# Merging attention's heads: the squares on ScalarE, the three turns of the reciprocal root and the scaled product on GpSimd

## The chip, the cores and the metric

The kernel runs on one core of a Trainium2 chip. The metric is the device time of one execution in microseconds (us). The engines are TensorE (PE, with its weight loads as PEld), VectorE (DVE), ScalarE (ACT), GpSimd (POOL) and SyncE (SP), which only issues transfers here.

## The reference

Two layers, each with a modulated layer norm, an attention-like part and a feed-forward part. Only the first layer's attention matters here: batch 8, 512 tokens, width 128, 16 heads, two softmax maps per head, values 16 wide.

```python
a1 = softmax(where(causal, s1, -inf)); a2 = softmax(where(causal, s2, -inf))
comb = a1 - lam[None, :, None, None] * a2
out = einsum('bhqk,bhkv->bhqv', comb, v)
mu = mean(out, -1); var = mean(square(out - mu), -1)
normed = (out - mu) * rsqrt(var + LN_EPS)
scaled = normed * (1.0 - LAM_INIT)
merged = scaled.transpose(0, 2, 1, 3).reshape(B, S, 2 * E)
return merged @ Wo
```

The kernel takes the mean out of the value weights beforehand, so `mu` is zero and only the mean of the squares is left to compute.

## The kernel before

Attention takes the first half of the execution. It goes in rounds of eight slots, `g` = 0 to 7, one round for each batch. A slot works on several things at once: the first pass of the scores for head pair `g` (matmuls into the banks `p1b`, and for each of ten units a row maximum by VectorE, `bmax`, L1055), the second pass for the pair two slots before (matmuls into `p2b`, exponentials by ScalarE into `pT`, L684), the causal clearing of `pT` by GpSimd (L645, twice a slot: once for blocks of the pair two slots before and once for the last blocks of the pair three slots before), the product with the values for the pair three slots before (`weigh`, L831), and the copying and turning of its result for the pair four slots before (L690, L861, L696).

The three banks `p1b` couple TensorE and VectorE closely: the second pair of units of a slot (units 2 and 3) can only be written once VectorE has read unit 0 of the same slot, the first pair only once it has read unit 8 of the slot before. At the end of a slot VectorE reduces the maxima to `qneg` (L1071). GpSimd splits that into `nsp` (L639, L641), and TensorE turns it in the middle of the next slot (L869, `turn_neg`). The turns all go through one bank, `auxb`, in a fixed order: `turn_neg`, `turn_o`, `value`, and each waits until ScalarE has copied out the one before.

Round r also finishes the batch `pb` = r - 1 ("post"). In slot 3 VectorE takes the reciprocals of the softmax sums (L1017). In slot 4 GpSimd makes the two scaled outputs `og` and `o2` (L655, L656), in slot 5 it adds them (L631). Then VectorE squares them before unit 4 of slot 5 (L1029), sums the squares before unit 8 of slot 5 (L1031), scales the sum and starts the reciprocal root before unit 4 of slot 6 (L1033 and L60 to L62), makes three Newton turns before units 5, 6 and 7 (L66 to L68) and the product `merged` before unit 9 (L1039). Each of the small steps waits for the one before through `Chain.link`. In slot 7 TensorE turns `merged` in two halves (`turn_m0` after the first pair of units, `turn_m1` after `weigh(1)`, L901), ScalarE copies them out (L719), and TensorE multiplies them with `wo` (L908). VectorE adds the gated result to `x` at the start of the next round (L1074, L1078).

On every engine the order is that of the program. GpSimd's order in a slot is: the copy of the values `vs` (L628), the addition of slot 5, `nsp`, the clearing of the last blocks, the post products of slot 4, and at the end of the slot the two clearings that wait for the eighth exponential. `weigh(1)` of the next slot waits for these:

```python
if c == CHUNK_FIRST:
    pe.wait_ge(masked, 2 * G + 2)
```

The last round, r = B = 8, has only post work of batch 7 left and does the whole of it on VectorE (`alone` on GpSimd is true then). Round 0 has no post work. So seven rounds, 1 to 7, have the steps above beside the other work.

Of the kernel before, what the change touches and what calls it, by code (L numbers as in the profile page):

```python
# [16 lines left out]
ALU = mybir.AluOpType  # L17
ACT = mybir.ActivationFunctionType
AX = mybir.AxisListType.X

B, S, D = 8, 512, 128
# [3 lines left out]
VD = 2 * HD  # L25
LAM_INIT = 0.8 - 0.6 * math.exp(-0.3 * 11)
EPS = 1e-5
# [15 lines left out]
class Chain:  # L43
# [6 lines left out]
    def link(self, ins):  # L50
        ins.then_inc(self.sem, 1)
        self.n += 1
        self.eng.wait_ge(self.sem, self.base + self.n)
        if self.passed is not None:
            self.eng.sem_inc(self.passed, 1)
# [376 lines left out]
GROUPS = 8  # L432
# [14 lines left out]
CHUNK_FIRST, CHUNK_LAST = 1, 0  # L447
O_COPY_AT, HIGH_AT, MT_AT, HT_AT, MID_AT, NEG_COPY_AT, OT_AT, V_COPY_AT = 0, 0, (1, 3), 2, 4, 4, 6, 9
RES_AT, NORM_AT = 3, 0
POST_AT = ((3, 9), (5, 4), (5, 8), (6, 4), (6, 5), (6, 6), (6, 7), (6, 9))  # L450
FIRST = ((DIAGONAL, 0), (EDGE, 0), (DIAGONAL, 1), (EDGE, 1), (MIDDLE, None))
BLOCK_STEP, SLOT_STEP, BLOCK_SLOTS, MAP_WORDS = 5, 2, 5, 28

# [35 lines left out]
def aux_use(r, g, kind):  # L489

    return (r + 1) * AUX_USES + AUX_PLACE[g, kind]
# [11 lines left out]
def attention(nc, d, k, t):  # L503
# [3 lines left out]
    with ExitStack() as ctx:  # L507
# [6 lines left out]
        def sem(name):  # L514
            return ctx.enter_context(nc.semaphore(name))
# [15 lines left out]
            sem(n) for n in ("first_unit", "first_read", "second_unit", "exp_done", "masked", "masked_last", "vs_ready", "av_done", "o_read"))  # L531
        qneg_ready, nsp_high, nsp_ready = (sem(n) for n in ("qneg_ready", "nsp_high", "nsp_ready"))
        rc_ready, og_ready, merged_ready, post_done = (sem(n) for n in ("rc_ready", "og_ready", "merged_ready", "post_done"))
        pool_own, dve_post, passed, og_parts = sem("pool_own"), sem("dve_post"), sem("passed"), sem("og_parts")
        f_xn, f_turned, f_hT, f_up, f_arg = (sem("f0_" + n) for n in ("xn", "turned", "hT", "up", "arg"))
        f_hid_tile, f_arg_tile, f_turns_tile = (tile[:, 0, :, :] for tile in ffn_tiles(k))
        f_bank, f_banks = p1b[0], (p1b[1], p1b[2], p2b[0], p2b[1])
# [74 lines left out]
        @block.gpsimd  # L612
        def _(pool):
            for s, n in CREDITS.items():
                pool.sem_inc(s, n)
            def slot(r, g, on, prep, post):
                pb = r - 1
                o = oT[:, (r + 1) % 2, :, :, 0:VD].rearrange("p c (h j) e -> p (c h) j e", j=2)
                rcv = rc[:, :, :, :].rearrange("p c h j -> p (c h) j")
                full = [P, TILES * H, VD]  # L620
                alone = isinstance(r, int) and r == B
                if on(2):
                    r2, g2 = lagged(r, g, 2)
                    G = r2 * GROUPS + g2
                    a = g2 % 2
                    pool.wait_ge(aux_read, aux_use(r2 - 1, 6, "value") + 1)
                    pool.wait_ge(av_done, G + 1)
                    pool.tensor_copy(vs[:, a, :, :, :], vst[:, r2 % 2, :, 2 * g2:2 * g2 + 2, :]).then_inc(vs_ready, 1)  # L628
                if post and g == 5 and not alone:
                    pool.wait_ge(pool_own, pb * 2 + 2)  # L630
                    pool.tensor_tensor(og[:, :, :], og[:, :, :], o2[:, :, :], ALU.add).then_inc(og_ready, 1)  # L631
                if on(1):
                    rn, gn = lagged(r, g, 1)
                    G, a = rn * GROUPS + gn, gn % 2
                    high, mid = (nsp[:, a, :, :, s, :].rearrange("p c j h -> p (c j) h") for s in range(2))
                    lowest = qneg[:, a, :, :].rearrange("p c (j h) -> p (c j) h", j=2)
                    pool.wait_ge(qneg_ready, G + 1)
                    pool.wait_ge(aux_done, aux_use(*lagged(r, g, 2), "turn_neg") + 1)
                    pool.tensor_copy(high, lowest).then_inc(nsp_high, 1)  # L639
                    pool.wait_ge(nsp_high, G + 1)  # L640
                    pool.tensor_tensor(mid, lowest, high, ALU.subtract).then_inc(nsp_ready, 1)  # L641

                def clear_future(pairs, n, signal):

                    pool.affine_select(out=pairs, in_=pairs, compare_op=ALU.is_ge, fill=0.0, base=0,  # L645
                                       pattern=[*n, [1, P]], channel_multiplier=-1).then_inc(signal, 1)

                if on(3):
                    r3, g3 = lagged(r, g, 3)
                    pool.wait_ge(exp_done, (r3 * GROUPS + g3 + 1) * UNITS + BANK_CREDITS)  # L650
                    clear_future(pT[:, g3 % 2, 8:10, :].rearrange("p n (a t) -> p (n a) t", a=2)[:, :, 0:P], [[0, 4]], masked_last)
                if post and g == 4 and not alone:
                    pool.wait_ge(rc_ready, pb + 1)
                    pool.wait_ge(merged_ready, pb + 1)
                    pool.tensor_tensor(og[:, :, :], o[:, :, 0, :], rcv[:, :, 0].unsqueeze(2).broadcast_to(full), ALU.mult).then_inc(pool_own, 1)  # L655
                    pool.tensor_tensor(o2[:, :, :], o[:, :, 1, :], rcv[:, :, 1].unsqueeze(2).broadcast_to(full), ALU.mult).then_inc(pool_own, 1)  # L656
                if prep and 1 <= g < 5:
                    j, J = g - 1, (r + 1) * 4 + g - 1
                    pool.wait_ge(mid_ready, J + 1)
                    pool.tensor_tensor(parts[:, j % 2, 2, :], res, parts[:, j % 2, 1, :], ALU.subtract).then_inc(split_ready, 1)  # L660
                if on(2):
                    r2, g2 = lagged(r, g, 2)
                    a = g2 % 2
                    pool.wait_ge(exp_done, (r2 * GROUPS + g2) * UNITS + 8 + BANK_CREDITS)
                    clear_future(pT[:, a, 0:8, 0:P], [[0, 8]], masked)
                    clear_future(pT[:, a, 1:8:2, 384:512], [[0, 4]], masked)

            rounds(pool, slot)

        @block.scalar  # L670
        def _(act):
            act.wait_ge(factor_ready, 1)

            def slot(r, g, on, prep, post):
# [6 lines left out]
                for u in range(UNITS):  # L681
# [22 lines left out]
                    if u == MID_AT and prep and 1 <= g < 5:  # L704
                        j = g - 1
                        act.wait_ge(aux_read, aux_use(r, g, "project") + 1)
                        act.activation(parts[:, j % 2, 1, :], res, ACT.Copy).then_inc(mid_ready, 1)
                    if u == NEG_COPY_AT and on(1):
                        rn, gn = lagged(r, g, 1)
                        act.wait_ge(aux_done, aux_use(r, g, "turn_neg") + 1)  # L710
                        if not isinstance(rn, int) or rn * GROUPS + gn >= 2:
                            rp, gp = lagged(rn, gn, 2)
                            act.wait_ge(neg_loaded[gp % RING], (use(rp, gp) + 1) * NEG_LOADS)
                        act.activation(nparts[:, gn % 2, :], auxb[0:2 * MAPS, 0:S // 2].bitcast(BF16), ACT.Copy).then_inc(aux_read, 1)
# [255 lines left out]
        def _(dve):  # L970
            fill = Chain(dve, dve_fill).link

            def slot(r, g, on, prep, post):
# [33 lines left out]
                        split_b2(dve, fill, k)  # L1007
                full = [P, TILES * H, VD]
                wide = lambda t: t[:, :].unsqueeze(2).broadcast_to(full)
                at = dict(zip(POST_AT[1:7], (0, 1, 2, 6, 9, 12)))  # L1010
                for u in range(UNITS):
                    if post and (g, u) in at:
                        link = Chain(dve, dve_post, pb * POST_LINKS + at[g, u]).link
                    if post and (g, u) == POST_AT[0]:
                        dve.wait_ge(aux_read, aux_use(r, POST_AT[0][0], "turn_o") + 1)
                        dve.wait_ge(og_ready, pb + 2)
                        dve.reciprocal(rc[:, :, :, :].rearrange("p c h j -> p c (h j)"), oT[:, (r + 1) % 2, :, :, VD]).then_inc(rc_ready, 1)  # L1017
                        if isinstance(r, int) and r == B:
# [5 lines left out]
                                dve.tensor_tensor(to[:, :, :], o[:, :, j, :], rcv[:, :, j].unsqueeze(2).broadcast_to(full), ALU.mult).then_inc(og_parts, 1)  # L1024
                            dve.wait_ge(og_parts, 2)
                            dve.tensor_tensor(og[:, :, :], og[:, :, :], o2[:, :, :], ALU.add).then_inc(og_ready, 1)
                    if post and (g, u) == POST_AT[1]:
                        dve.wait_ge(og_ready, pb + 3)
                        link(dve.tensor_tensor(sq[:, :, :], og[:, :, :], og[:, :, :], ALU.mult))  # L1029
                    if post and (g, u) == POST_AT[2]:  # L1030
                        link(dve.tensor_reduce(vsum[:, :], sq[:, :, :], AX, ALU.add))  # L1031
                    if post and (g, u) == POST_AT[3]:
                        link(dve.tensor_scalar(vsum[:, :], vsum[:, :], 1.0 / VD, EPS, ALU.mult, ALU.add))  # L1033
                        rsqrt_start(dve, link, vsum[:, :], vhalf[:, :], orstd[:, :], otmp[:, :])
                    if post and (g, u) in POST_AT[4:7]:
                        rsqrt_newton(dve, link, vhalf[:, :], orstd[:, :], otmp[:, :])
                    if post and (g, u) == POST_AT[7]:
                        dve.wait_ge(aux_done, aux_use(r - 1, GROUPS - 1, "turn_m1") + 1)
                        dve.scalar_tensor_tensor(merged[:, :, :].rearrange("p c (h e) -> p (c h) e", e=VD), og[:, :, :], 1.0 - LAM_INIT,  # L1039
                                                 wide(orstd), ALU.mult, ALU.mult).then_inc(merged_ready, 1)  # L1040
                    if on(0):
                        t, j = divmod(u, 2)
                        kind, head = FIRST[t]
# [36 lines left out]
            rounds(dve, slot)  # L1080


POST_LINKS = 3 + RSQRT_LINKS


def token_stats(dve, link, k, batches):
# [1378 lines left out]
```

## Time and profile before

| what | value |
|---|---|
| median of 3 runs | 1449.06 us (1448.51 to 1450.49) |
| profiled execution | 1447.97 us, span 1446.2 us |
| attention in the trace | from about 57 us to about 680 us |
| PE / DVE / ACT / POOL busy over the span | 83% / 80% / 74% / 55% |
| mean granted clock of TensorE | 0.939 |

The profiled execution lies 1.09 us below the median of the runs. 1.8 us of it lie outside the span. The shares of busy time are averages over stages with different limits; the rows below come from single slots of attention.

### The profile page before, as it was taken

The page shows a single profiled execution, that of the slowest core. Times are in us where ns is not written, and L with a number is a line of the kernel's source. Part 1 is how long each engine was busy: PE and PEld are TensorE (multiplying, and loading weights), DVE is VectorE, ACT ScalarE, POOL GpSimd, SP SyncE. Part 2 cuts the span into 40 slices and gives each one's busy share as a digit, 9 for nine tenths or more (in the row PEclk, how much of TensorE's full clock was granted, in tenths as well). Part 3 has the DMA queues.
Part 4 walks back from the last instruction along what each step waited for, and adds up shares of the span by engine and source line. Part 5 has one row for each costly group of instructions (what it writes and reads, how often), then busy time and mean ns, then how long its engine had stood idle before and what let it go on. Part 6 is the DMA issues. An engine that isn't in the chain of part 4 may idle for free. (4 is left out here: it accounts for less than half of the span.)

```text
span 1446.2 us, 26470 instructions
## 1 busy us (share of the span) xinstructions
PE 1200.6 (83%) x8837; PEld 562.0 (39%) x8837; DVE 1156.0 (80%) x2000; ACT 1072.2 (74%) x1712; POOL 801.6 (55%) x721
## 2 busy tenths in 40 slices
PE   4489989898989898876876678787669999999998
PEld 3234443434444444333544223232234444444443
DVE  5678988888888888886776999999947776777653
ACT  2178878787878787874976888885467788778775
POOL 3134636362636363530001699899637787777777
PEclk8589999999999999996898899998889999999999
DMA  5341414141414141100003798988578677767884
GB/s 134 101 133 55 135 36 143 35 141 39 137 42 136 44 133 46 57 3 0 1 0 97 242 298 312 300 284 283 177 157 186 174 193 179 192 174 184 191 199 120
DMA packets 123690, 198.63 MB, mean 137 GB/s; under 512 B 24604, under 2 KB 60088, under 8 KB 123576
## 3 DMA queue, kind: packets, MB, share of 16 engines
q1 hardware_dynamic: 122136, 195.08, 47.4%
q10 hardware_dynamic: 1440, 2.10, 0.5%
q8 instruction: 64, 1.05, 0.3%
q14 instruction: 50, 0.41, 0.1%
HBM read 167.76 MB, written 28.84 MB: 136 GB/s over the span
## 5 line engine op out<-in xcount | busy, mean ns | idle before, releaser
L1055 DVE TENSOR_REDUCE bmax<-p1b 128x4 f32<-128x512 f32 x640 | 406.9, 685 | 64.0 <-PE p1b L760 58.2
L684 ACT ACTIVATE pT<-p2b 128x512 f32<-128x512 f32 x640 | 349.3, 599 | 97.5 <-PE p2b L813 97.3
L2203 POOL TENSOR_TENSOR hid_l<-e_hid,w_experts 128x1024 f16<-128x1024 f32 (+1 forms) x136 | 281.1, 2083 | 104.5 <-ACT w_experts L2338 103.6
L645 POOL TENSOR_SCALAR_AFFINE_SELECT pT<-pT 128x512 f32<-128x512 f32 (+1 forms) x192 | 148.0, 787 | 201.9 <-ACT pT L684 201.9
L2437 DVE TENSOR_TENSOR e_hid<-ub,w_experts 128x1024 f32<-128x1024 f32 x128 | 155.8, 1223 | 121.7 <-ACT ub L2349 113.1
L831 PE MATMUL ob<-pT,vs 128*32 128x384 f32 (+3 forms) x2048 | 185.7, 447 | 8.3 <-ACT o_sb L690 6.5
L1906 PE MATMUL yb<-ch,ident 128*128 128x512 f32 x256 | 134.5, 655 | 45.8 <-POOL ch L1876 45.5
L2338 ACT ACTIVATE w_experts<-e_hid 128x1024 f16<-128x1024 f32 (+1 forms) x136 | 139.4, 1026 | 38.3 <-DVE e_hid L2437 38.2
L2349 ACT ACTIVATE ub<-ub 128x1024 f32<-128x1024 f32 (+1 forms) x136 | 133.9, 985 | 37.6 <-PE ub L2254 35.9
L760 PE MATMUL p1b<-w_high 48*128 48x128 bf16 (+2 forms) x1792 | 129.0, 246 | 37.3 <-DVE bmax L1055 37.1
L813 PE MATMUL p2b<-w_high 50*128 50x512 bf16 (+3 forms) x1024 | 124.8, 301 | 2.4 <-ACT pT L684 1.9
L1986 ACT ACTIVATE dA<-dt,nA 128x511 f32<-128x511 f32 x128 | 85.5, 712 | 46.7 <-DVE hs L2049 34.7
L2252 PE MATMUL ub<-w,w_high 128*128 (+1 forms) x264 | 100.9, 382 | 22.2 <-DVE e_hid L2437 12.9
L760 PEld LDWEIGHTS p1b<-w_high 48*128 48x128 bf16 x1792 | 63.4, 96 | 115.6 <-DVE bmax L1055 97.7
L1876 POOL TENSOR_TENSOR ch<-hs,crow 128x1024 f32<-128x1024 f32 x40 | 93.9, 2353 | 12.6 <-DVE hs L2049 12.5
L2253 PE MATMUL ub<-w,w_high 128*128 (+1 forms) x264 | 100.8, 382 | 0.0
L2254 PE MATMUL ub<-w,w_low 128*128 (+1 forms) x264 | 100.8, 382 | 0.0
L2252 PE MATMUL e_yb<-w_experts,w_high 128*128 128x512 f16 x264 | 100.1, 379 | 0.5 <-POOL hid_l L2203 0.5
L2254 PE MATMUL e_yb<-w_experts,w_low 128*128 128x512 f16 x264 | 100.1, 379 | 0.0
L2253 PE MATMUL e_yb<-hid_l,w_high 128*128 128x512 f16 x264 | 100.1, 379 | 0.0
L1906 PEld LDWEIGHTS yb<-ch,ident 128*128 128x128 f32 x256 | 47.2, 200 | 121.7 <-POOL ch L1876 76.3
L2049 DVE TENSOR_TENSOR_SCAN hs<-dA,dBx 128x1024 f32<-128x1024 f32 x40 | 91.4, 2284 | 3.4 <-ACT dA L1986 0.6
(308 smaller groups left out, 2150.4 us busy)
## 6 DMA issues: line engine op xcount, KB each, us to landing
w_experts<-shares SPq DMA_DIRECT2D x256, 256.0 KB, 4.3
brow<-bc_rows SPq DMA_DIRECT2D x64, 512.0 KB, 4.0
crow<-bc_rows SPq DMA_DIRECT2D x64, 512.0 KB, 5.3
q_stacks<-w_low SPq DMA_DIRECT2D x96, 128.0 KB
k_stacks<-w_low SPq DMA_DIRECT2D x96, 128.0 KB
w_high<-q_stacks SPq DMA_DIRECT2D x128, 96.0 KB, 2.4
w_high<-k_stacks SPq DMA_DIRECT2D x128, 96.0 KB, 2.3
w_high<-nparts SPq DMA_DIRECT2D x128, 4.0 KB
```

Source lines behind the costliest of these rows:

```text
L645: pool.affine_select(out=pairs, in_=pairs, compare_op=ALU.is_ge, fill=0.0, base=0, pattern=[*n, [1, P]], channel_multiplier=-1).then_inc(s ...
L684: act.activation(pT[:, g2 % 2, stored(u), :], p2b[bank_of(g2, u)][:, :], ACT.Exp, scale=SCALE).then_inc(exp_done, 1)
L760: return pe.matmul(bank[:, at * P:(at + blocks[1] - blocks[0]) * P], qs[rows, slot, head, c * P:(c + 1) * P], ks[rows, slot, head, blocks[ ...
L831: mm = pe.matmul(ob[32 * m:32 * m + 32, q0:q1], vs[:, a, c, m // 2, :], pT[:, a, u, at:at + q1 - q0], start=(c == CHUNK_FIRST), stop=(c == ...
L1055: dve.tensor_reduce(to, bank, AX, ALU.max).then_inc(first_read, 1)
L1906: mm = pe.matmul(yb[:, :], k.ident[:, :], ch[:, m % 4, j, :], start=False, stop=(m == PAIRS - 1 and j == 1), skip_group_check=True)
L2203: pool.tensor_tensor(flat(hid_l[:, rounded(p), 0:n, :]), flat(hid[:, place(p), 0:n, :]), rounded_half(p, 0, n), ALU.subtract).then_inc(spl ...
L2252: pe.matmul(to, w[0], high, start=start, stop=False, skip_group_check=True)
L2253: pe.matmul(to, w[0], low, start=False, stop=False, skip_group_check=True)
L2254: return pe.matmul(to, w[1], high, start=False, stop=stop, skip_group_check=True)
L2338: act.activation(rounded_half(p, 0, n), flat(hid[:, place(p), 0:n, :]), ACT.Copy).then_inc(hid_rounded, 1)
L2437: dve.tensor_tensor(h, u, flat(share[:, p % SHARES, :, :]), ALU.mult).then_inc(hid_ready, 1)
```

## The change

ScalarE squares `og` in slot 5 after its fifth exponential (`SQ_AT`). VectorE sums the squares before unit 7 of slot 5, and scales the sum and starts the root before unit 9 of slot 5. GpSimd makes the three turns, as twelve chained instructions instead of nine, and the product, in slot 6 between the clearing of the last blocks and the two clearings at the end. The factor 1 - LAM_INIT goes into the scale of the sum, so that the last product is a plain one. The last round keeps everything on VectorE, at other places of the program but in the same sequence.

```diff
-POST_AT = ((3, 9), (5, 4), (5, 8), (6, 4), (6, 5), (6, 6), (6, 7), (6, 9))
+SQ_AT = 4
+RC_AT, SUM_AT, START_AT, MERGE_AT = (3, 9), (5, 7), (5, 9), (6, 6)
+MERGE_SCALE = (1.0 - LAM_INIT) ** -2
...
+                if post and g == 6 and not alone:
+                    pool.wait_ge(dve_post, (pb + 1) * POST_LINKS)
+                    link = Chain(pool, pool_newton, pb * NEWTON_LINKS).link
+                    for _ in range(3):
+                        link(pool.tensor_tensor(otmp[:, :], orstd[:, :], orstd[:, :], ALU.mult))
+                        link(pool.tensor_tensor(otmp[:, :], otmp[:, :], vhalf[:, :], ALU.mult))
+                        link(pool.tensor_scalar(otmp[:, :], otmp[:, :], 1.5, None, ALU.add))
+                        link(pool.tensor_tensor(orstd[:, :], orstd[:, :], otmp[:, :], ALU.mult))
+                    pool.wait_ge(aux_done, aux_use(r - 1, GROUPS - 1, "turn_m1") + 1)
+                    pool.tensor_tensor(merged[:, :, :].rearrange("p c (h e) -> p (c h) e", e=VD), og[:, :, :],
+                                       orstd[:, :].unsqueeze(2).broadcast_to(full), ALU.mult).then_inc(merged_ready, 1)
...
+                    if post and (g, u) == (5, SQ_AT) and not (isinstance(r, int) and r == B):
+                        act.wait_ge(og_ready, pb + 3)
+                        act.activation(sq[:, :, :], og[:, :, :], ACT.Square).then_inc(sq_ready, 1)
...
-                    if post and (g, u) == POST_AT[1]:
-                        dve.wait_ge(og_ready, pb + 3)
-                        link(dve.tensor_tensor(sq[:, :, :], og[:, :, :], og[:, :, :], ALU.mult))
-                    if post and (g, u) == POST_AT[2]:
+                    if post and (g, u) == SUM_AT:
+                        dve.wait_ge(sq_ready, pb + 1)
                         link(dve.tensor_reduce(vsum[:, :], sq[:, :, :], AX, ALU.add))
-                    if post and (g, u) == POST_AT[3]:
-                        link(dve.tensor_scalar(vsum[:, :], vsum[:, :], 1.0 / VD, EPS, ALU.mult, ALU.add))
+                    if post and (g, u) == START_AT:
+                        link(dve.tensor_scalar(vsum[:, :], vsum[:, :], MERGE_SCALE / VD, MERGE_SCALE * EPS, ALU.mult, ALU.add))
                         rsqrt_start(dve, link, vsum[:, :], vhalf[:, :], orstd[:, :], otmp[:, :])
-                    if post and (g, u) in POST_AT[4:7]:
-                        rsqrt_newton(dve, link, vhalf[:, :], orstd[:, :], otmp[:, :])
-                    if post and (g, u) == POST_AT[7]:
+                    if post and (g, u) == MERGE_AT and isinstance(r, int) and r == B:
+                        for _ in range(3):
+                            rsqrt_newton(dve, link, vhalf[:, :], orstd[:, :], otmp[:, :])
```

## Rows read from the trace of the kernel before

**Rows 1.** Windows, from a slot's first score matmul to the next slot's; columns: PE, PEld, DVE, ACT, POOL busy, clock.

```profile
110.01:118.12 8.11, 7.31 (x98) 3.42 (x94) 6.50 (x11) 6.88 (x15) 2.97 (x7) 1.00 0.20 59
241.47:250.92 9.45, 7.64 (x98) 3.38 (x95) 8.25 (x12) 7.05 (x15) 6.56 (x8) 1.00 0.45 144
250.92:261.36 10.44, 7.42 (x94) 3.48 (x95) 9.89 (x25) 7.00 (x14) 3.57 (x8) 1.00 0.17 47
261.36:272.38 11.02, 9.91 (x118) 5.85 (x118) 9.10 (x16) 7.83 (x15) 2.68 (x5) 1.00 0.18 49
624.25:636.81 12.56, 12.47 (x117) 6.90 (x118) 9.19 (x16) 7.78 (x15) 2.68 (x5) 0.75 0.01 2
```

**Rows 2.** Windows over slots 7 and 0, from `qneg` to `qneg`, rounds 1 and 2.

```profile
189.12:208.56 19.44, 17.52 (x203) 9.21 (x204) 15.70 (x29) 14.12 (x28) 5.01 (x10) 0.91 0.09 25
263.06:281.29 18.23, 16.25 (x202) 8.72 (x204) 15.61 (x29) 14.10 (x28) 5.01 (x10) 1.00 0.10 27
```

**Rows 3.** Timeline of PE, round 2: start, us, instruction, idle before it and its releaser.

```profile
258.44 0.39 PE L760 MATMUL p1b<-w_high 48*128 48x256 bf16 x4 [1.55 <-DVE bmax L1055]
...
261.36 0.39 PE L767 MATMUL p1b<-identb,later 64*128 64x256 bf16 x4 [0.69 <-DVE bmax L1055]
...
262.40 0.66 PE L901 MATMUL auxb<-ident,merged 128*128 128x128 f32 x4 [0.20 <-DVE merged L1039]
263.95 0.39 PE L760 MATMUL p1b<-w_high 48*128 48x384 bf16 x4 [0.89 <-DVE bmax L1055]
```

**Rows 4.** Timeline of VectorE, round 2, slots 5 and 6.

```profile
244.69 1.22 DVE L1029 TENSOR_TENSOR sq<-og 128x1024 f32<-128x1024 f32 x1
...
248.84 1.21 DVE L1031 TENSOR_REDUCE vsum<-sq 128x64 f32<-128x1024 f32 x1
...
254.03 0.18 DVE L1033 TENSOR_SCALAR vsum<-vsum 128x64 f32<-128x64 f32 x1
...
254.94 0.69 DVE L1055 TENSOR_REDUCE bmax<-p1b 128x4 f32<-128x512 f32 x1
...
258.30 0.74 DVE L66 TENSOR_TENSOR otmp<-orstd 128x64 f32<-128x64 f32 x1
```

**Rows 5.** Timeline of VectorE and of PE, round 0, a slot without post work.

```profile
115.21 2.49 DVE L1055 TENSOR_REDUCE bmax<-p1b 128x4 f32<-128x512 f32 x4 [0.22 <-PE p1b L760]
...
111.41 0.39 PE L760 MATMUL p1b<-w_high 48*128 48x384 bf16 x4 [0.57 <-DVE bmax L1055]
```

**Rows 6.** Timeline of ScalarE, round 2, slot 5.

```profile
245.37 0.60 ACT L684 ACTIVATE pT<-p2b 128x512 f32<-128x512 f32 x1 [0.34 <-PE p2b L813]
246.47 0.59 ACT L714 ACTIVATE nparts<-auxb 8x512 bf16<-8x512 bf16 x1 [0.51 <-PE auxb L869]
```

**Rows 7.** Groups of ScalarE instructions, by form: shapes and functions near the new Square.

```profile
L2338 ACT ACTIVATE w_experts<-e_hid 128x1024 f16<-128x1024 f32 x128 | 134.5, 1051 | 38.3 <-DVE e_hid L2437 38.2
L1300 ACT ACTIVATE factor_tile<-ee,front_constants 128x512 f32<-128x512 f32 x28 | 18.5, 707 | 0.0
```

**Rows 8.** Timeline of GpSimd, round 2: end of slot 5, start of slot 6.

```profile
249.40 1.68 POOL L645 TENSOR_SCALAR_AFFINE_SELECT pT<-pT 128x1024 f32<-128x1024 f32 x2 [2.81 <-ACT pT L684]
...
251.79 0.20 POOL L639 CAST nsp<-qneg 128x16 bf16<-128x16 f32 x1 [0.37 <-DVE qneg L1071]
252.07 0.22 POOL L641 TENSOR_TENSOR nsp<-qneg,nsp 128x16 bf16<-128x16 f32 x1
252.25 0.63 POOL L645 TENSOR_SCALAR_AFFINE_SELECT pT<-pT 128x512 f32<-128x512 f32 x1
...
257.88 1.68 POOL L645 TENSOR_SCALAR_AFFINE_SELECT pT<-pT 128x1024 f32<-128x1024 f32 x2 [5.00 <-ACT pT L684]
```

**Rows 9.** Groups of GpSimd instructions, by form.

```profile
L655 POOL TENSOR_TENSOR og<-w_experts,rc 128x1024 f32<-128x1024 f32 x7 | 13.8, 1965 | 0.0
```

**Rows 10.** Timeline: VectorE's scalar form on SBUF beside GpSimd's clearing, last round.

```profile
644.90 0.49 DVE L1117 TENSOR_SCALAR half<-stats 128x28 f32<-128x28 f32 x1
...
644.73 0.63 POOL L645 TENSOR_SCALAR_AFFINE_SELECT pT<-pT 128x512 f32<-128x512 f32 x1
```

More of the change, by code:

```diff
@@ L533, in attention @@
         rc_ready, og_ready, merged_ready, post_done = (sem(n) for n in ("rc_ready", "og_ready", "merged_ready", "post_done"))
-        pool_own, dve_post, passed, og_parts = sem("pool_own"), sem("dve_post"), sem("passed"), sem("og_parts")
+        pool_newton = sem("pool_newton")
+        pool_own, dve_post, og_parts, sq_ready = sem("pool_own"), sem("dve_post"), sem("og_parts"), sem("sq_ready")
         f_xn, f_turned, f_hT, f_up, f_arg = (sem("f0_" + n) for n in ("xn", "turned", "hT", "up", "arg"))
@@ L1009, in slot @@
                 wide = lambda t: t[:, :].unsqueeze(2).broadcast_to(full)
-                at = dict(zip(POST_AT[1:7], (0, 1, 2, 6, 9, 12)))
+                at = dict(zip((SUM_AT, START_AT, MERGE_AT), (0, 1, 5)))
                 for u in range(UNITS):
@@ L1013, in slot @@
                         link = Chain(dve, dve_post, pb * POST_LINKS + at[g, u]).link
-                    if post and (g, u) == POST_AT[0]:
-                        dve.wait_ge(aux_read, aux_use(r, POST_AT[0][0], "turn_o") + 1)
+                    if post and (g, u) == RC_AT:
+                        dve.wait_ge(aux_read, aux_use(r, RC_AT[0], "turn_o") + 1)
                         dve.wait_ge(og_ready, pb + 2)
@@ L1026, in slot @@
                             dve.tensor_tensor(og[:, :, :], og[:, :, :], o2[:, :, :], ALU.add).then_inc(og_ready, 1)
-                    if post and (g, u) == POST_AT[1]:
-                        dve.wait_ge(og_ready, pb + 3)
-                        link(dve.tensor_tensor(sq[:, :, :], og[:, :, :], og[:, :, :], ALU.mult))
-                    if post and (g, u) == POST_AT[2]:
+                            dve.wait_ge(og_ready, pb + 3)
+                            dve.tensor_tensor(sq[:, :, :], og[:, :, :], og[:, :, :], ALU.mult).then_inc(sq_ready, 1)
+                    if post and (g, u) == SUM_AT:
+                        dve.wait_ge(sq_ready, pb + 1)
                         link(dve.tensor_reduce(vsum[:, :], sq[:, :, :], AX, ALU.add))
-                    if post and (g, u) == POST_AT[3]:
-                        link(dve.tensor_scalar(vsum[:, :], vsum[:, :], 1.0 / VD, EPS, ALU.mult, ALU.add))
+                    if post and (g, u) == START_AT:
+                        link(dve.tensor_scalar(vsum[:, :], vsum[:, :], MERGE_SCALE / VD, MERGE_SCALE * EPS, ALU.mult, ALU.add))
                         rsqrt_start(dve, link, vsum[:, :], vhalf[:, :], orstd[:, :], otmp[:, :])
-                    if post and (g, u) in POST_AT[4:7]:
-                        rsqrt_newton(dve, link, vhalf[:, :], orstd[:, :], otmp[:, :])
-                    if post and (g, u) == POST_AT[7]:
+                    if post and (g, u) == MERGE_AT and isinstance(r, int) and r == B:
+                        for _ in range(3):
+                            rsqrt_newton(dve, link, vhalf[:, :], orstd[:, :], otmp[:, :])
                         dve.wait_ge(aux_done, aux_use(r - 1, GROUPS - 1, "turn_m1") + 1)
-                        dve.scalar_tensor_tensor(merged[:, :, :].rearrange("p c (h e) -> p (c h) e", e=VD), og[:, :, :], 1.0 - LAM_INIT,
-                                                 wide(orstd), ALU.mult, ALU.mult).then_inc(merged_ready, 1)
+                        dve.tensor_tensor(merged[:, :, :].rearrange("p c (h e) -> p (c h) e", e=VD), og[:, :, :], wide(orstd), ALU.mult).then_inc(merged_ready, 1)
                     if on(0):
@@ L1080, in _ @@
             rounds(dve, slot)
-POST_LINKS = 3 + RSQRT_LINKS
+POST_LINKS = 2 + 3
+NEWTON_LINKS = 12
 def token_stats(dve, link, k, batches):
```

## The prediction

> **What bounds the kernel now.** I read the windows by slot first. A slot of round 0 with no post work lasts 8.11 us from its first score matmul to the next slot's, with VectorE busy 6.50 us of it. In round 2, with post work, slot 5 lasts 9.45, slot 6 10.44 and slot 7 11.02 us [rows 1]. Slots 5 and 6 hold the same TensorE work as the 8.11 us slot; slot 7 has the turns of `merged` and the product with `wo` as well. The timeline of TensorE then says what the extra time is: it waits for `bmax`, 1.55 us before the last pair of slot 6, 0.69 us before slot 7's first pair and 0.89 us before its second [rows 3]. So in slots 5 to 7 the end is set by VectorE, which is late by the post steps it does between the maxima [rows 4]; elsewhere the two run in step, TensorE waiting 0.57 us for the round trip of the first read [rows 5]. Third, TensorE's clock: slots 7 and 0 take 18.23 us at the full 2.4 GHz in round 2, and 19.44 us in round 1 at a mean granted clock of 0.91 [rows 2], the low level of 1.2 GHz being granted for a part of slot 7. I found slot 7 slowed in rounds 1, 3, 5 and 7, and in round 7 slot 7 alone takes 12.56 instead of 11.02 us at 0.75 [rows 1]. Each time it follows the waits of slot 6.
>
> **The change, part by part, worked out in round 2.** Two small edits cost nothing: the factor folded into the sum's scale, and round 8, where the same chain stays on VectorE with the same instructions.
>
> *The square on ScalarE.* The near row is an ACTIVATE of 1024 f32 columns at 1.05 us [rows 7]; with the overlap of neighbours I take 0.95. Bounds are 0.71, the 512-column Square, and 1.4, twice that. The 28 Squares of the scan stand among exponentials and carry no table load of their own [rows 7], so I charge none. The fifth exponential starts at 245.37, and `nparts` now starts only at 246.47 because it waits for `nsp`, which waited for VectorE's square [rows 6]. With the square on ScalarE, `nparts` can start at 245.87 + 0.95 = 246.8, 0.35 later than before. The rest of ScalarE's slot was packed with small idle times, so the eighth exponential and the clearing by GpSimd stay at about 249.4 [rows 8]. On TensorE the delay is hidden behind the wait for VectorE below.
>
> *VectorE in slot 5.* Gone is the square, 1.22 us; the sum, 1.21 us, moves ahead of unit 7; the scale and start, from 254.03 to 254.94, 0.91 us, come ahead of unit 9 [rows 4]. In the plain slot the last four reads begin 5.20 us after the first matmul (115.21 less 110.01) [rows 1, 5], so here at 246.7. One read to 247.3, the sum to 248.5 (its input is ready at 246.8), reads of units 7 and 8 to 249.7. Now the four scalar instructions stand beside GpSimd's two clearings, 249.40 to 251.08 [rows 8]. The trace shows what becomes of them: in the last round a scalar instruction of 28 columns took 0.49 us and ended with a clearing begun at 644.73 [rows 10], and the Newton step that met the clearing of 257.88 took 0.74 us [rows 4, 8], where the scale of the sum, of the same width and alone, took 0.18 [rows 4]. So I put the first to 250.5, when the first clearing ends, the second to 251.1, when the second ends, and the last two to 251.6. Read of unit 9 to 252.2, `qneg` to 252.5, the read of unit 0 of slot 6 to 253.1, and TensorE's second pair of slot 6 at 253.2. Without that collision it would be 252.2. Both ends stay for the range: 1.0 us a round.
>
> The Trainium skill, "SBUF — State Buffer", section "Who interferes with whom", has the same as a rule: GpSimd and a VectorE scalar instruction in a two-port mode take one pair of ports as an exclusive lock, and a reduce never does. The trace agrees (0.49 us above). By that rule the sum and the maxima are free of it and the start of the root is not, which gives the 1.0 us; without it the sum of this prediction would be 7 us lower.
>
> *Slot 6.* No post work is left on VectorE. From the second pair to the next slot the plain slot takes 118.12 - 111.41 = 6.71 us [rows 1, 5], so slot 7 begins at 253.2 + 6.7 = 259.9 instead of 261.36: 1.45 us gained.
>
> *GpSimd in slot 6.* Nothing in the trace is a chained GpSimd step of 64 columns. From the copy of 16 columns at 251.79 to the chained subtraction at 252.07 are 0.28 us, with 0.20 busy, so 0.08 us of hand-over [rows 8]. From 16 to 1024 columns a two-input operation grows from 0.22 to 1.965 us [rows 8, 9], 1.73 ns a column, so 64 columns take 0.30, and 0.38 with the hand-over; the one-input step I take at 0.32. Three turns are 9 × 0.38 + 3 × 0.32 = 4.4 us. Bounds are 12 × 0.28 = 3.4 us, and 12 × 0.71 = 8.5 us if a small step costs what the clearing of 512 columns does (0.63 plus the hand-over) [rows 8]. I take 4.4, since the small rows are nearest. It begins after `qneg`, `nsp` and the last-block clearing: 252.5 + 0.2 + 0.45 + 0.63 = 253.8, ends at 258.2, and the product of 1.97 us [rows 9] at 260.2. TensorE asks for `merged` after slot 7's first pair, at 259.9 + 0.75 = 260.65. Queued behind the product are the two clearings, 1.68 us [rows 8], now to 261.9; `weigh(1)` asks for them at about 262.15. Both just fit, with 0.3 to 0.4 us to spare. The next `vs`, `nsp` and their users are over a microsecond further off.
>
> *Slot 7.* The waits of 0.69, counted already, and of 0.20 for `merged` and 0.89 us for `bmax` [rows 3] go, since VectorE is on time; some 0.3 us for ScalarE's copy `o_sb` remain, which the later wait had covered. Gain 0.8 us.
>
> *The clock.* Slowed slots cost 3 × 1.21 + 1.54 = 5.2 us in all [rows 1, 2]. The waits that come before them shrink in slots 6 and 7, but one of about 1.9 us arises before slot 6's second pair (251.35 to 253.2). I take half of it back, 2.6 us.
>
> **The sum.** 7 rounds × (1.45 + 0.8) = 15.75, and 2.6: 18.3 us. From the profiled execution's 1447.97 that gives 1429.6; the median of the runs stands 1.09 above, so 1430.7 us.
>
> **Rivals.**
>
> *No collision.* If VectorE's start of the root isn't held up, by the clearings being later or by these forms not taking the lock, each round gains 1.0 us more: 1423.7, and 1421.1 with the whole of the clock. For it: `L1033` and its neighbours took 0.18 to 0.20 us in the trace, with no clearing beside them [rows 4]. Against: the 0.49 us [rows 10], and the clearing's place at 249.40.
>
> *The clock doesn't recover, or GpSimd is a little late.* If all seven rounds pay about 1.21 us, the clock term is -3.3 in place of +2.6, near 1436.6. If a step takes 0.12 us more than I reckon, 12 × 0.12 - 0.3 = 1.1 us a round come back: 1438.7.
>
> *GpSimd becomes the bound.* This is the one that ends slower. The chain of twelve and the product stand ahead of the clearings, and both `turn_m0` and `weigh(1)` wait behind it. Each round loses 12 times what a step costs above 0.37, less 0.3 us. It eats the 2.6 us a round (gain and clock) when a step takes 0.61 us; at 0.71 the loss is 12 × 0.34 - 0.3 = 3.8 us a round, with the clock term lost too 1447.97 + 1.09 + 7 × (3.8 - 2.25) = 1459.9. Against it: 0.28 us from step to step at 16 columns, and the maxima of slot 6, which read PSUM and left GpSimd's times alone.
>
> The Trainium skill, "GPSIMD Engine Reference", section "4.1 Engine selection", speaks for this rival: elementwise work belongs on VectorE, since GpSimd is about two times slower with two inputs. The product agrees, 1.97 us on GpSimd. The rule prices the engine alone; GpSimd is idle 5.00 us ahead of the clearing in slot 6 [rows 8], which holds most of the 6.4 us.
>
> *Nothing.* The saved time could be given back in slot 0, whose length is set by VectorE's gating, norm and reads. Against it: these begin only after `wo`, which comes earlier.
>
> **Chances.** The forecast with the collision, 1426 to 1435: 0.50. No collision, below 1426: 0.20. Late GpSimd or clock, up to 1446: 0.19. Within 0.2%, about 3 us and about what a measurement can tell from no change: 0.04. GpSimd bound, slower: 0.07. So faster 0.89, same 0.04, slower 0.07. The range goes from 1421 (no collision, whole clock) to 1440 (late GpSimd); little above it is in, so it leaves out under 2 in 10.
>
> **What would show it.** Slot 6 should last about 9 us and slot 7 about 10.2, from first matmul to first matmul. VectorE's four instructions of the start should show 0.5 us or more for two of them, and the second pair of slot 6 should wait near 1.9 us. A turn on GpSimd should take 1.5 us, and `turn_m0` and `weigh(1)` of slot 7 should wait for nothing on GpSimd. ScalarE should show no new table load. Wrong would be: steps of over 0.5 us on GpSimd, a wait for `merged` or for the clearing on TensorE, or `nparts` late enough that `turn_o` holds TensorE up in slot 5.

## The result, and the profile after

The changed kernel takes 1439.32 us (median of 6 runs, 1435.74 to 1444.08) against 1450.12 us for the kernel before in the same comparison (6 runs, 1448.51 to 1453.36). The ratio is 0.9924, 95% interval 0.9908 to 0.9939: faster by about 11 us, or 0.8%. The forecast was 1430.7 us, the range 1421 to 1440: the measured time lies in the range, but 8.6 us above the forecast and 0.7 us below the upper end. The profiled execution took 1435.74 us, its span is 1434.0 us, 12.2 us less than before. One execution of the changed kernel, in experiment 10, took 1743.82 us at a mean granted clock of 0.643, and its time is left out of the ratio given there.

The windows of round 2 after, from a slot's first score matmul to the next slot's, for slots 5, 6 and 7, and then slot 6 cut in three (columns as in rows 1, the clock third from the right):

```profile
238.86:247.73 8.87, 7.47 (x99) 3.28 (x96) 7.31 (x12) 7.63 (x16) 5.32 (x8) 1.00 0.45 145
247.73:258.50 10.77, 8.76 (x98) 3.92 (x95) 8.39 (x16) 7.03 (x14) 8.29 (x19) 0.84 0.14 39
258.50:268.86 10.36, 9.93 (x122) 5.86 (x118) 7.37 (x13) 7.64 (x16) 3.97 (x8) 1.00 0.23 67
247.73:251.15 3.42, 1.41 (x26) 0.74 (x22) 3.21 (x8) 1.66 (x3) 1.92 (x6) 0.98 0.27 83
251.15:254.50 3.35, 3.35 (x35) 1.48 (x37) 2.00 (x4) 1.50 (x3) 2.69 (x9) 0.51 0.02 5
254.50:258.50 4.00, 4.00 (x47) 1.70 (x40) 3.19 (x6) 3.87 (x9) 3.67 (x6) 1.00 0.12 30
```

Beside [rows 1]: slot 5 went from 9.45 to 8.87 us, slot 7 from 11.02 to 10.36, and slot 6, which holds none of VectorE's post work any more, from 10.44 to 10.77. The last three rows show why: TensorE is busy 1.41 us of the first 3.42, and the next 3.35 us run at a clock of 0.51, the low level of 1.2 GHz. The timeline of TensorE in slots 5 and 6 has the waits:

```profile
244.91 0.63 PE L878 MATMUL auxb<-ident,o_sb 128*128 128x128 f32 x4 [0.60 <-ACT nparts L731]
...
250.57 0.39 PE L777 MATMUL p1b<-w_high 48*128 48x384 bf16 x4 [2.01 <-DVE bmax L1071]
250.80 0.42 PE L830 MATMUL p2b<-w_high 50*128 50x384 bf16 x4
251.15 1.51 PE L848 MATMUL ob<-pT,vs 128*32 128x384 f32 x8
...
260.75 0.85 PE L848 MATMUL ob<-pT,vs 128*32 128x384 f32 x8 [0.23 <-ACT o_sb L704]
```

The 2.01 us are the wait that replaced those of 1.55, 0.69 and 0.89 us [rows 3]; `weigh(1)` behind it takes 1.51 us, where it takes 0.85 at the full clock in slot 7. VectorE, in the same stretch:

```profile
244.74 1.21 DVE L1048 TENSOR_REDUCE vsum<-sq 128x64 f32<-128x1024 f32 x1
245.98 1.29 DVE L1071 TENSOR_REDUCE bmax<-p1b 128x4 f32<-128x512 f32 x2
247.19 0.50 DVE L1050 TENSOR_SCALAR vsum<-vsum 128x64 f32<-128x64 f32 x1
247.72 0.55 DVE L60 TENSOR_SCALAR otmp<-vsum 128x64 int32<-128x64 int32 x1
248.30 0.31 DVE L61 TENSOR_SCALAR orstd<-otmp 128x64 int32<-128x64 int32 x1
248.65 0.20 DVE L62 TENSOR_SCALAR vhalf<-vsum 128x64 f32<-128x64 f32 x1
248.88 0.69 DVE L1071 TENSOR_REDUCE bmax<-p1b 128x4 f32<-128x512 f32 x1
249.68 0.24 DVE L1087 TENSOR_REDUCE qneg<-bmax 128x16 f32<-128x80 f32 x1
```

The four steps from 247.19 take 1.69 us up to the next read, where they took 0.91 [rows 4]. Beside the first two stand GpSimd's two clearings, 246.54 to 248.22, and beside the third its copy of `vs`, 248.17 to 248.57. GpSimd, from there to the product:

```profile
246.54 1.68 POOL L648 TENSOR_SCALAR_AFFINE_SELECT pT<-pT 128x1024 f32<-128x1024 f32 x2 [3.47 <-ACT pT L698]
...
251.04 0.29 POOL L668 TENSOR_TENSOR otmp<-orstd 128x64 f32<-128x64 f32 x1
251.41 0.32 POOL L669 TENSOR_TENSOR otmp<-otmp,vhalf 128x64 f32<-128x64 f32 x1
251.82 0.37 POOL L670 TENSOR_SCALAR otmp<-otmp 128x64 f32<-128x64 f32 x1
252.27 0.32 POOL L671 TENSOR_TENSOR orstd<-orstd,otmp 128x64 f32<-128x64 f32 x1
252.67 0.29 POOL L668 TENSOR_TENSOR otmp<-orstd 128x64 f32<-128x64 f32 x1
...
255.92 1.93 POOL L673 TENSOR_TENSOR merged<-og,orstd 128x1024 f32<-128x1024 f32 x1
257.81 1.68 POOL L648 TENSOR_SCALAR_AFFINE_SELECT pT<-pT 128x1024 f32<-128x1024 f32 x2
```

A turn takes 1.63 us, three 4.88, and everything is done at 259.5; in slot 7 TensorE waits for none of it. ScalarE's square:

```profile
243.25 1.05 ACT L724 ACTIVATE sq<-og 128x1024 f32<-128x1024 f32 x1
244.20 0.57 ACT L731 ACTIVATE nparts<-auxb 8x512 bf16<-8x512 bf16 x1
```

In rounds 1 to 6 slot 7 is 10.35 or 10.36 us, none slowed, and slot 6 is 10.69 to 10.83 us, all slowed; so is slot 6 of round 7, which has less work (10.46 us at a clock of 0.84; 8.94 at 1.00 in experiment 3). A slot is called slowed here where its granted clock is below 1.00 for a part of it.

### The profile page after: what moved, and what is told of

Its sections match the earlier page's. It is cut to its first block and busy times, and to the rows that moved or that the text cites. A ratio compares the mean times of both kernels' runs of the same rounds, so it can differ in the third digit from the quotient of the medians.

```text
span 1434.0 us, 26470 instructions
## 1 busy us (share of the span) xinstructions
PE 1198.4 (84%) x8837; PEld 561.1 (39%) x8837; DVE 1126.1 (79%) x1923; ACT 1074.9 (75%) x1719; POOL 834.9 (58%) x812
## 3 DMA queue, kind: packets, MB, share of 16 engines
q10 hardware_dynamic: 1440, 2.10, 0.5%
q8 instruction: 64, 1.05, 0.3%
## 5 line engine op out<-in xcount | busy, mean ns | idle before, releaser
L663 POOL TENSOR_TENSOR w_low<-w_low 128x512 bf16<-128x512 f32 x32 | 38.3, 1197 | 97.7 <-ACT w_low L721 97.7
```

## The experiments

Each is told with its edit against the changed kernel, if not said otherwise. The ratios are to the kernel before, run on the same chip. Experiments 1 to 4 ran on one chip, 5, 7, 8 and 9 on a second, 6 and 10 on a third, so between these groups the ratios are compared. In the diffs, `...` stands for lines left out.

**1. The start of the root behind slot 6's first read.**

```diff
-RC_AT, SUM_AT, START_AT, MERGE_AT = (3, 9), (5, 7), (5, 9), (6, 6)
+RC_AT, SUM_AT, START_AT, MERGE_AT = (3, 9), (5, 7), (6, 1), (6, 6)
```

> The scale of the sum and the start of the root go from ahead of unit 9 of slot 5 to ahead of unit 1 of slot 6, behind the read of unit 0. Theory (the four scalar instructions meet GpSimd's clearings and make the first read of slot 6 late; the 2.0 us wait that this leaves TensorE with is what drops the clock): the four take 0.8 us instead of 1.6, the wait ahead of the second pair of slot 6 falls from 2.0 to about 0.6 us, a wait of about 0.5 us arises before the third pair, the clock stays at its high level, slot 6 lasts about 8.7 us instead of 10.8, and the time is near 1424. Rival (the clock falls whatever that wait is, because slots 5 to 7 hold several waits): slot 6 near 9.9, time near 1432. Rival (GpSimd's chain is next in line and takes over): TensorE waits for merged or for the clearing in slot 7, and the time stays above 1434.

Measured: 1428.66 us (5 runs, 1428.23 to 1430.65), ratio 0.9855 (0.9834 to 0.9875). Slots 5 and 6 of round 3 (windows), TensorE's waits in slot 6, and VectorE's first step:

```profile
310.32:319.19 8.87, 7.47 (x98) 3.27 (x95) 7.34 (x11) 7.63 (x16) 5.32 (x8) 1.00 0.45 144
319.19:328.26 9.07, 7.38 (x99) 3.42 (x96) 8.14 (x17) 6.85 (x14) 7.18 (x18) 1.00 0.16 46
```

```profile
320.59 0.39 PE L777 MATMUL p1b<-w_high 48*128 48x384 bf16 x4 [0.57 <-DVE bmax L1071]
...
323.18 0.39 PE L784 MATMUL p1b<-identb,later 64*128 64x256 bf16 x4 [0.89 <-DVE bmax L1071]
...
320.45 0.66 DVE L1050 TENSOR_SCALAR vsum<-vsum 128x64 f32<-128x64 f32 x1
```

The first wait is that of the plain slot. The second, before the third pair, is 0.89 us where some 0.5 was expected, because the first of the four steps still meets a clearing (that of the last blocks, 320.43 to 321.06) and takes 0.66 us. Slot 6 lasts 9.07 us in four of rounds 1 to 6 and 8.74 in round 4, where slot 5 took 9.20 and the step met less of the clearing (0.33 us). Round 2 was slowed all the same, 10.61 us, behind waits no longer than those shown. GpSimd's chain begins 2.7 us into slot 6, where it began at 3.3 with the start in slot 5 (VectorE being done with slot 5 sooner), and nothing waits for it, so the rival of GpSimd falls; that of the clock too, by the 9.07 us. The place of four small steps was worth 10 us. At the high clock it is worth little, 9.25 (experiment 3) less 9.07 us a round, some 1.3 us in all; the rest is the clock, which stayed up in six rounds of seven.

**2. The sum later too.**

```diff
+RC_AT, SUM_AT, START_AT, MERGE_AT = (3, 9), (6, 1), (6, 2), (6, 6)
```

> The sum goes to unit 1 of slot 6 and the start to unit 2: slot 5 of VectorE holds no post work at all. Theory: slot 6 can hide only about 0.5 to 0.8 us of VectorE's work behind its first read, so the third pair waits some 1.5 us, and GpSimd's chain begins 1.3 us later, which uses up its spare time: about 1 to 2 us a round slower than the kernel with only the start moved, near 1434. Rival (VectorE has ample idle time in slot 6, 1.5 us in the plain slot): as fast as the kernel with only the start moved.

Measured: 1440.22 us (1438.31 to 1442.54), ratio 0.9936 (0.9915 to 0.9956). TensorE waits 1.67 us before the third pair instead of 0.89, and slot 6 of round 3 runs at 0.85:

```profile
324.53 0.39 PE L784 MATMUL p1b<-identb,later 64*128 64x256 bf16 x4 [1.67 <-DVE bmax L1071]
```

That is 11.6 us more than experiment 1, 1.7 us a round, in the expected 1 to 2. Round 1, the one of rounds 1 to 6 that kept the high clock, has a slot 6 of 9.85 us, 0.8 more than 9.07, and a wait of 0.26 us for `merged` behind it; the others take 11.2 to 12.5 us at clocks of 0.73 to 0.85. So here too more than half of the loss is the clock. VectorE's idle time in a slot is spread over gaps, and only what fits behind one read is free.

**3. Five turns instead of three on GpSimd.**

```diff
-                    for _ in range(3):
+                    for _ in range(NEWTON_LINKS // 4):
...
-NEWTON_LINKS = 12
+NEWTON_LINKS = 20
```

> GpSimd makes five turns instead of three, 20 chained steps instead of 12; all else as in the changed kernel. The result is the same root, turned twice more. Theory (three turns fit with about 1.2 us to spare, merged being done at 257.8 and the clearing at 259.5, while TensorE asks at 259.3 and 260.8): 8 steps of 0.405 us are 3.2 us, less 1.2 spare, about 2 us a round, 14 us in all, near 1453. Rival (GpSimd has much more room): under 5 us. Rival (GpSimd already sets the end): the whole 3.2 us a round, 23 us.

Measured: 1460.87 us (4 runs, 1458.79 to 1462.87), ratio 1.0077 (1.0052 to 1.0103), some 22 us slower than the changed kernel. In round 3 the product ends at 338.96 and TensorE asked for it 3.39 us earlier:

```profile
328.39 0.39 PE L777 MATMUL p1b<-w_high 48*128 48x384 bf16 x4 [2.01 <-DVE bmax L1071]
...
339.01 0.66 PE L918 MATMUL auxb<-ident,merged 128*128 128x128 f32 x4 [3.39 <-POOL merged L673]
340.65 1.50 PE L848 MATMUL ob<-pT,vs 128*32 128x384 f32 x8 [0.44 <-POOL pT L648]
```

So GpSimd's chain sets the end once it outgrows its slot, and it brings its own low clock. The expected 2 us a round were too few: the low clock follows this wait as well, and the spare time of 1.2 us holds only where slot 6 is slowed: 3.39 us less the 3.27 that eight steps take leaves 0.1, so with three turns and a slot 6 at the high clock GpSimd would be just late. The windows of slot 6 in rounds 2 and 3 of this one execution show that, and price the clock:

```profile
250.98:261.76 10.78, 8.77 (x99) 4.10 (x96) 8.40 (x16) 7.04 (x14) 7.80 (x24) 0.84 0.14 39
325.54:334.79 9.25, 7.24 (x98) 3.38 (x95) 8.39 (x16) 6.96 (x14) 6.60 (x20) 1.00 0.16 46
```

Round 3 has the same wait of 2.01 us (first line above) and stays at the high clock. The low clock costs 10.78 less 9.25, 1.53 us, and such a wait does not bring it every time.

**4. The wait filled with matmuls.** After the first pair of slot 6:

```diff
+                if post and g == 6 and not (isinstance(r, int) and r == B):
+                    pe.wait_ge(aux_read, aux_use(r, 5, "value") + 1)
+                    for _ in range(3):
+                        pe.matmul(auxb[:, :], k.ident[:, :], hT, start=True, stop=True)
```

> Three extra matmuls of 512 f32 columns by TensorE, into the free bank auxb, ahead of the second pair of slot 6, where the changed kernel waits 2.0 us; their result is not used. They take about 1.95 us. Theory (the wait drops the clock, and the low clock costs 1.2 us in each of seven rounds): the clock of slot 6 reads 1.00, slot 6 lasts about 9.6 us, and the time falls by 8 us to near 1431, although TensorE has more to do. Rival (the long slot 6 has another cause, and the low clock costs nothing by itself): the time stays or grows by up to 1 us a round.

Measured: 1431.47 us (1429.2 to 1433.78), ratio 0.9873 (0.9851 to 0.9894).

```profile
249.37 2.84 PE L964 MATMUL auxb<-w_low,ident 128*128 128x512 f32 x6
...
248.61:258.55 9.94, 9.94 (x104) 4.45 (x100) 8.49 (x16) 6.95 (x14) 7.46 (x18) 1.00 0.14 41
```

The three took 2.84 us, more than the wait, and slot 6 is 9.94 us in each of rounds 1 to 6 at a clock of 1.00: 9.25 plus the 0.7 by which they run over. The granted clock is 1.00 in round 7 too. With more work on TensorE the kernel is 7 to 8 us faster than the changed kernel. That is the shown cause of most of the gap to the forecast: the low clock behind the wait.

**5. The square earlier.** As experiment 1, and `SQ_AT = 3`.

> As the kernel with the start behind the first read of slot 6, and the square on ScalarE one exponential earlier (after the fourth, not the fifth, of slot 5). Theory (the square on ScalarE makes nparts late, and with it turn_o, which TensorE waits 0.60 us for in slot 5): the wait in slot 5 goes, slot 5 lasts 8.3 us instead of 8.87, and the time falls by 3.5 to 4 us to near 1425. Rival (the wait was hidden by VectorE's sum, which keeps the last reads late anyway): slot 5 gets shorter and slot 6 as much longer, no change.

Measured: 1428.78 us (6 runs, 1421.23 to 1433.06), ratio 0.9849 (0.9826 to 0.9872). In the profiled execution, of 1421.23 us, the wait of 0.60 for `nparts` is gone, slot 5 lasts 8.56 us and slot 6 8.96 in each of rounds 1 to 6, none slowed. But the start still meets GpSimd's clearing of the last blocks, 387.00 to 387.67, and the third pair waits 0.80 us:

```profile
386.99 0.18 DVE L1050 TENSOR_SCALAR vsum<-vsum 128x64 f32<-128x64 f32 x1
387.21 0.51 DVE L60 TENSOR_SCALAR otmp<-vsum 128x64 int32<-128x64 int32 x1
```

Slots 5 and 6 take 17.52 us together, 0.42 less than in experiment 1, where 0.57 was expected; the median is that of experiment 1, inconclusive, with a spread of 12 us.

**6. The same with two waits filled,** one matmul of 512 columns before the second and one before the third pair of slot 6.

> The kernel with the square earlier and the start later, with one extra matmul of 512 f32 columns by TensorE ahead of the second and one ahead of the third pair of slot 6, where it waits 0.6 and 0.8 us; their result is not used. Theory (its runs spread from 1421 to 1433 us because the clock falls in slot 6 in some rounds of some executions): the runs lie closer together and their median falls to near 1423. Rival (the low clock strikes elsewhere in these executions): spread and median stay, 1429.

Measured: 1427.43 us (5 runs, 1424.49 to 1428.83), ratio 0.9836 (0.982 to 0.9851), the lowest ratio of all. The spread is 4.3 us instead of 12, and no slot 6 is slowed, at 9.28 or 9.29 us each. The median is only 1.4 us lower, the matmuls cost 0.3 us a round, and the intervals of experiments 1, 5 and 6 overlap. This was run on another chip than experiment 5, whose profiled execution had no slowed slot 6 either, so the narrower spread is not shown to be their doing.

**7. Only the square moved.** The kernel before, with the square on ScalarE (the code of the change) and the rest on VectorE in its old places.

> Of the change only the square on ScalarE, after the fifth exponential of slot 5; the sum, the start, the turns and the product are on VectorE where the kernel before has them. Theory: slot 5 lasts 8.9 us instead of 9.45, slot 6 stays near 10.4 since the turns and the product are still there, about 0.5 to 1 us a round, 1443 to 1447. Rival (the square is the part that carries the gain): near 1440.

Measured: 1446.04 us (10 runs, 1440.14 to 1449.47), ratio 0.9954 (0.9936 to 0.9971): some 6 us. Slot 5 lasts 8.87 us, slot 6 10.44 in four of rounds 1 to 6 and up to 11.11 in the others, and two rounds still have a slot 7 of 12.45.

**8. The square back on VectorE,** turns and product on GpSimd.

> The changed kernel with the square back on VectorE, ahead of unit 4 of slot 5; the turns and the product stay on GpSimd. Theory (slot 5 is where VectorE is late, and each microsecond there counts nearly in full): the wait for nparts goes, but the second pair of slot 6 comes about 1 us later still, near 1446. Rival (the square was worth its whole 1.22 us): 1448. Rival (the lateness of nparts costs as much as the square saves): no change to the changed kernel, 1439.

Measured: 1443.98 us (7 runs, 1437.9 to 1446.23), ratio 0.9943 (0.9923 to 0.9963). Slot 5 lasts 9.46 us again, slot 6 9.14 where the clock is high and 10.6 to 12.0 where it fell (five of rounds 1 to 6). At the high clock, in round 2, GpSimd's clearing comes late: `weigh(1)` of slot 7 waits 0.44 us for it, 0.2 more than elsewhere for `o_sb`. Apart the two halves, the square alone (experiment 7) and the turns and product alone (this one), give about 6 and 8 us, together 11; the interval of this one overlaps that of the changed kernel.

**9. The kernel before with its wait filled,** two matmuls of 512 columns before the last pair of slot 6, with the wait for `turn_o`'s copy.

> The kernel before, with two extra matmuls of 512 f32 columns by TensorE ahead of the last pair of slot 6, where it waits 1.55 us for VectorE; their result is not used. They take 1.3 us. Theory (in the kernel before too it is this wait that brings the low clock to slot 7 in four of seven rounds): no round has a slow slot 7, and the time falls by up to 5 us to near 1445. Rival (the low clock of slot 7 comes from the waits of slot 7 itself, 0.69, 0.20 and 0.89 us): no change, or 1 to 2 us slower.

Measured: 1445.76 us (12 runs, 1443.47 to 1450.97), ratio 0.9965 (0.9951 to 0.9979). Slot 6 of round 2 lasts 10.53 us and slot 7 10.92, at a clock of 1.00, and so in all of rounds 1 to 6:

```profile
260.01:270.93 10.92, 9.91 (x122) 5.83 (x118) 9.00 (x16) 7.83 (x15) 3.59 (x6) 1.00 0.21 64
```

```profile
262.50 0.39 PE L760 MATMUL p1b<-w_high 48*128 48x384 bf16 x4 [0.89 <-DVE bmax L1059]
```

The two matmuls took 1.98 us instead of the expected 1.3 and made TensorE later, so the waits of 0.69 and 0.20 us behind them are gone in rounds 1 to 6 with most of the 1.55; the 0.89 us in slot 7 stand. So the slowed slots 7 of the kernel before hung on the waits from the last pair of slot 6 on, and not on the 0.89 us alone. Which of them it was this run doesn't separate.

**10. The changed kernel again.**

> The changed kernel once more, on the chip and in the rounds of the run beside it, for a comparison on one chip. Theory: near 1439, with the low clock in slot 6 of every round, since the wait of 2.0 us there is the same each time. Rival (which rounds are slowed is chance): some rounds of slot 6 at 9.6 us.

Measured: a ratio of 0.9915 (0.9901 to 0.9929) from 5 runs of 1437.22 to 1440.71 us. The time repeats. The only trace is of the execution of 1743.82 us, so which rounds were slowed stays open here.

## Why the prediction was right in part

The measured time is in the range, but the most likely outcome, 1426 to 1435, was missed, and the time stayed inside only because the range reached up for rivals given 0.19; with 0.7 us to the end of the range that is partly luck. The steps at the high clock were right; the clock was not. Step by step, in round 2:

- *The square.* Right: 1.05 us, 0.95 to the next instruction, no table load. `nparts` held `turn_o` up by 0.60 us in slot 5, named as a way to be wrong. In the changed kernel it is hidden, as the prediction said: VectorE has no idle time over 0.15 us from 244.13 to 252.31, and TensorE waits 2.01 us for it afterwards. It counts once the start stands later: experiment 5 got 0.4 us of it back over slots 5 and 6 (17.94 to 17.52).
- *The collision.* Right in kind, a little too dear: 0.78 us lost instead of 1.0, since two of the four steps were held up by some 0.3 us each (they ended at 247.68 and 248.27, the clearings at 247.64 and 248.22) and a third by 0.1. The wait it feeds was put at 1.9 us and is 2.01.
- *Slot 6.* Slots 5 and 6 were to last from 241.47 to 259.9, 18.4 us. With the 9.25 us of a slot 6 at the high clock (experiment 3) they are 18.1, since from the second pair on the slot takes 6.4 us and not the 6.7 of the plain slot; in the changed kernel's profile they are 19.6.
- *GpSimd.* Steps of 0.41 us on the average, the one-input step at 0.45 the longest, against 0.38 and 0.32; 4.88 us for 4.4. It fitted, with 1.0 to 1.4 us to spare, but only because slot 6 was slowed; at the high clock the 0.3 to 0.4 us foreseen (0.45 and 0.25 by the prediction's own times) were not there (0.1 us late by experiment 3, and a wait of 0.44 us in round 2 of experiment 8). The rival that it becomes the bound needed steps of 0.61 us; experiment 3 shows that the mechanism is real, with 8 more steps.
- *Slot 7.* 10.36 for 10.2; the waits named are gone.
- *The clock.* This is the term that failed: the prediction took back half of the 5.2 us, 2.6 us, on the ground that the waits before the slowed slots shrink, and the new wait of 1.9 us that it named beside them counted only as the other half not regained, not as a cost of its own. The slowed slots 7 did all go, 3 × 1.45 + 1.54 = 5.9 us from slot to slot, but slot 6 was slowed in every round, 7 × 1.5 = 10.5 us: -4.6 in place of +2.6. Filling that wait gave 7 to 8 us (experiment 4). The rival of the clock had this, at 0.19 together with a late GpSimd, and 1436.6 us.

The sum by the measured terms: 30.91 less 8.87, 9.25 and 10.36 is 2.43 us a round, 17.0 for seven, less 4.6, 12.4; the span fell by 12.2. The profiled execution, 1435.74 us, is 6.1 us above the 1429.6 that the prediction gives for it. The other 2.5 us of the distance to 1430.7 are that the changed kernel's median stands 3.6 us above its profiled execution, the fastest of its runs, and the kernel before's 1.1 in the times that the forecast had. The five other runs have mean granted clocks of 0.927 to 0.936 against 0.937; where in them the clock was lower no trace shows.

The expected gain was thus made, and some 5 us of it given back by the clock behind the one long wait that the change put in the place of several short ones.

## What to carry to other kernels

Where two engines hand banks to each other, taking work off the late one pays only as far as its last read before a hand-over comes sooner; ask which read the next matmul needs, and put small steps behind it, not before it (10 us here for four instructions, most of it through the clock). Several short waits merged into one long one can cost more than they save, because TensorE's clock may fall behind the long one (1.5 us a time here, for a wait of 2.0 us). A helper engine with much idle time is free until its chain reaches the next consumer; compute that point from the end of what must come first, and for the slot at its fastest, not slowed.

## What the runs showed of the hardware

- Integer scalar steps of VectorE are held up by GpSimd's clearing as float ones are: 0.55 and 0.51 us for an int32 step that takes 0.20 alone. The maxima beside it were not (1.29 us for two, as elsewhere), nor the sum (1.21 us at 248.84 in the kernel before, beside the clearing of 249.40).
- Chained GpSimd steps of 64 columns take 0.37 to 0.45 us from start to start, and a one-input step with a constant (0.37 us busy) is slower than a two-input one (0.29 to 0.32). VectorE's two-input step of this width took 0.22 us, and the product 1.22 us against GpSimd's 1.93.
- Whether the low clock follows a wait differs between rounds of one execution. Counted over the seven rounds of each profiled execution, slot 6 was slowed in 7 (changed kernel) and in 2 (experiment 3) behind the same 2.0 us, in 6 behind 1.89 (experiment 8), in 5 behind 1.67 (experiment 2), in 1 behind 0.57 and 0.89 (experiment 1), in none behind 0.62 and 0.80 (experiment 5), and in none of 14 where the waits were filled (experiments 4 and 6). The runs of one kernel spread by 2 to 12 us; that this is the clock's doing is likely, but not shown.
